# Attention scores in one round over four banks, x standardised by GpSimd, the gate bias over 128 rows, and a new order at the end of a step

## The chip, the cores and the metric

The kernel runs on one core of a Trainium2 chip. The metric is the device time of one launch in microseconds; lower is better. Times of single operations below come from one profiled execution.

## The reference, cut to what matters

One transformer layer over 4096 tokens of 256 numbers: a gated linear attention with 16 heads of 16, and then a mixture of eight experts of which each token uses two.

```python
h = layernorm(x) * (1 + ca) + sa
q, k, v = h @ Wq, h @ Wk, h @ Wv                       # 16 heads of 16
g = log_sigmoid(h @ Wgk1 @ Wgk2 + bgk2) / 16
state_t = state_{t-1} * exp(g_t) + v_t k_t^T           # a scan over the tokens, for each head
o_t = state_t q_t
o = (layernorm(o) * gamma + beta) * silu(h @ Wg)
x = x + ga * (o @ Wout)
h2 = layernorm(x) * (1 + cb) + sb
w = softmax over the two best of (h2 @ Wr + br)        # eight experts
x = x + gb * sum_e w_e * (gelu(h2 @ W1[e] + b1[e]) @ W2[e] + b2[e])
```

## The kernel before, in words

The tokens are cut into 32 chunks of 128. The scan is done by chunks: inside a chunk as a masked product of scores with values, between chunks by a 256-wide state. The heads lie in four strips of 32 partitions (two heads in a strip for each of the two halves j of the 256 numbers).

The program is five instruction streams (SyncE, GpSimd, ScalarE, VectorE, TensorE). Each is written out by hand as a function `step(s, u, front, back, finish, route)`, and `walk` (line 412) calls it for s = -1 to 33. Steps 4 to 29 are a loop of 13 rounds with two steps each; the others are written out. Each engine works strictly in its own order, and semaphores bind the streams. In one step s four chunks are at different stages:

- front (chunk f = s+1): projections of h to gate and decay (`p_gz`, with a bias product of `ones_r` by `zb_r` over two rows), to q and k (`p_qk`) and to v (`p_v`), their transposes, and the cumulative sums of the decay (`p_cum`). Each float32 product of h is made as three of rounded parts. `hT_lo_r` (line 873, VectorE) is the low part of h.
- back (chunk s): scores (line 1125), their mask (line 863), outputs (line 1138), the update of the state.
- finish (chunk s-1): normalisation of the output (lines 880 and 883), the product with Wout, the residual x1 (line 911), and its standardisation into `rows` (line 956).
- route (chunk s-2): the router's scores (line 899), the two best experts (lines 901 to 921), places of rows (lines 965 to 985), and two indirect DMAs (line 635).
- nextx (chunk s+2): statistics of x (line 894), the inverse root on ScalarE (line 739), the standardised x on VectorE (line 928, whose instruction is recorded at line 809, tile `host_n`), its transposes on TensorE, and h on ScalarE (line 764).

PSUM has eight banks: `p_tr`, `p_qk`, `p_v`, `p_gz`, `p_cum`, `p_o` and the two of `p_s`. The scores of strips 0 and 1 are made in the two banks of `p_s`; VectorE masks them into SBUF (`mask(0)`); then the scores of strips 2 and 3 are made in the same two banks and masked (`mask(1)`). TensorE puts the gate projection between the two rounds. The last things on TensorE in a step are the transposes of x, the transposes of `rows` into `p_v`, the counts of the router into `p_cum`, and the transposes of the output into `p_o`.

After the 34 steps VectorE makes tables, and 64 to 72 tiles of 128 rows go through the experts. That stage reuses the same banks and is not touched.

In the rows, all products have line 1099 and the transposes 1118, so a tile's name tells them apart: `p_s<-w_all,qkT_both` are scores, `w_hi<-p_s,upto` is a mask, `host_n<-host_x,mv_x` is x standardised, `w_r<-hT,w_r` is the low part of h, `p_gz<-zb_r,ones_r` the bias product, and `w_all<-qkT_both,own_pair` (line 599, GpSimd) is `qbd`, the left operand of the next step's scores.

## Time and profile before

| | us |
|---|---|
| median of three runs | 957.5 (956.02 to 960.76) |
| the profiled execution's own time | 960.28 |
| its span, first to last instruction | 958.1 |
| TensorE busy | 877.5 (92%) |
| VectorE busy | 626.1 (65%) |
| ScalarE busy | 473.4 (49%) |
| GpSimd busy | 403.7 (42%) |
| mean granted TensorE clock | 0.965 |

The profile calls TensorE PE (its weight loads PEld), VectorE DVE, ScalarE ACT, GpSimd POOL and SyncE SP. A busy share is an average over stages with different limits; the steps of attention and the tiles of the experts have to be read apart. A PE row's time ends when its last result is written, so the time that an operation takes on TensorE is better read from one start to the next.

### The profile page before, as it was taken

The numbers are of one execution on the slowest core, as the hardware profiler recorded it, in microseconds if no ns is written. First come the engines' busy times: TensorE is split into PE (matmuls) and PEld (weight loads), VectorE is DVE, ScalarE is ACT, GpSimd is POOL, SyncE is SP. The second block draws the span as 40 slices with busy tenths as digits, with TensorE's granted clock in tenths as the row PEclk, the third lists the DMA queues.
The fourth block names the chain that finished last, engine by engine and source line by source line (L and its number), as shares of the span: only waits on it lengthen the run. The fifth ranks groups of instructions, "written<-read, shape, count | busy, mean of one in ns | idle before, by whom it ended". The sixth has DMA issues, their size and how long they took to land.

```text
span 958.1 us, 24566 instructions
## 1 busy us (share of the span) xinstructions
PE 877.5 (92%) x6743; PEld 751.3 (78%) x6744; DVE 626.1 (65%) x1478; ACT 473.4 (49%) x1425; POOL 403.7 (42%) x419
## 2 busy tenths in 40 slices
PE   5799999999999999998269999999999999999995
PEld 4477777777777777776269999999999999999994
DVE  2578888888888888886534747465474565645653
ACT  2366666666666666663134443444434444443441
POOL 2246555555555555554204343343334434243342
PEclk9699999999999999998579999999999999999997
DMA  6911111111111111111273222222222222222222
GB/s 238 379 57 58 47 55 56 49 47 52 48 56 56 42 53 50 50 51 41 76 277 65 39 45 34 45 40 39 45 34 45 40 39 40 39 45 40 40 36 25
DMA packets 51449, 62.64 MB, mean 65 GB/s; under 512 B 6274, under 2 KB 46932, under 8 KB 51284
## 3 DMA queue, kind: packets, MB, share of 16 engines
q1 hardware_dynamic: 38548, 44.36, 14.4%
q0 software_dynamic: 12864, 17.83, 10.9%
q8 instruction: 17, 0.28, 0.1%
q14 instruction: 20, 0.16, 0.1%
HBM read 38.91 MB, written 23.27 MB: 65 GB/s over the span
## 4 chain that ended last, share of the span: by engine, by line
PE 70%; DVE 13%; issue 10%; DVEq 2%; ACT 2%; DMA 1%; SPq 1%; POOL 0%; ACTq 0%; POOLq 0%
PE p_s L1099 24%; PE p_qk L1099 11%; PE p_gz L1099 10%; PE p_v L1099 9%; PE p_cum L1099 6%; PE p_o L1099 4%; PE p_tr L1099 2%; DVE rows L809 2%; DVE w_hi L867 2%; PE p_o L1118 2%; PE p_v L1118 1%; PE p_tr L1279 1%; DMA w_all<-in_L_wmod_dram 1%; DVE o_tok L970 1%; DVE host_s_r L1083 1%
## 5 line engine op out<-in xcount | busy, mean ns | idle before, releaser
L655 POOL DMA_INDIRECT out_dram<-x,tok x68 | 166.6, 2450 | 312.5 <-DVE x L1076 297.0
L674 ACT ACTIVATE h2T<-p_tr,mods 128x128 f32<-128x128 f32 x136 | 54.9, 454 | 259.0 <-PE p_tr L1279 246.4
L1099 PE MATMUL p_s<-w_all_r,host_s_r 128*128 x544 | 143.1, 405 | 2.9 <-DVE host_s_r L1083 2.9
L1099 PEld LDWEIGHTS p_s<-w_all_r,host_s_r 128*128 128x128 f32 x544 | 97.8, 190 | 20.8 <-issue 3.3
L599 POOL TENSOR_TENSOR w_all<-qkT_both,own_pair 128x512 f32<-128x512 f32 x32 | 33.2, 1037 | 139.0 <-ACT qkT_both L744 139.0
L867 DVE TENSOR_TENSOR w_hi<-p_s,upto 128x1024 f32<-128x1024 f32 x64 | 77.9, 1218 | 12.2 <-PE p_s L1099 12.2
L635 POOL DMA_INDIRECT expert_rows<-rows,pos x64 | 64.4, 1006 | 49.7 <-issue 32.3
L1072 DVE TENSOR_TENSOR ga<-p_s,b_all 128x256 f32<-128x256 f32 x68 | 28.8, 423 | 85.3 <-PE p_s L1099 85.1
L1099 PE MATMUL p_s<-w_all,qkT_both 32*128 32x256 f32 x512 | 73.9, 406 | 3.6 <-DVE w_hi L867 1.5
L1099 PE MATMUL p_qk<-h2T,host_x 128*128 128x128 f32 x544 | 68.3, 280 | 2.5 <-ACT h2T L674 1.0
L1099 PE MATMUL p_v<-h2T,host_x 128*128 128x128 f32 x544 | 67.1, 276 | 3.3 <-DVE qkT_both L1035 2.4
L1099 PEld LDWEIGHTS p_qk<-h2T,host_x 128*128 128x128 f32 x544 | 65.4, 196 | 3.4 <-issue 3.4
L1099 PEld LDWEIGHTS p_v<-h2T,host_x 128*128 128x128 f32 x544 | 63.6, 192 | 4.7 <-issue 4.1
L1099 PE MATMUL p_cum<-h2T,qkT_both 128*128 128x128 f32 x544 | 66.8, 276 | 0.0
L1099 PE MATMUL p_gz<-h2T,qkT_both 128*128 128x128 f32 x544 | 66.3, 275 | 0.0
L1099 PEld LDWEIGHTS p_cum<-h2T,qkT_both 128*128 128x128 f32 x544 | 64.0, 193 | 0.0
L1099 PEld LDWEIGHTS p_gz<-h2T,qkT_both 128*128 128x128 f32 x544 | 63.5, 192 | 0.0
L1069 DVE CAST tok<-ln_host 128x1 uint32<-128x1 f32 x68 | 10.4, 153 | 75.9 <-issue 75.9
L1099 PEld LDWEIGHTS p_s<-w_all,qkT_both 32*128 32x128 f32 x512 | 44.5, 186 | 17.9 <-DVE w_hi L867 8.4
L1099 PE MATMUL p_gz<-w_r 128*128 128x512 f32 x128 | 46.2, 443 | 12.7 <-DVE w_hi_r L848 7.6
L723 ACT ACTIVATE host_s<-p_gz 128x512 f32<-128x512 f32 x32 | 19.1, 598 | 54.6 <-PE p_gz L1099 54.6
L1099 PEld LDWEIGHTS p_gz<-w_r 128*128 128x128 f32 x128 | 21.3, 194 | 30.8 <-DVE w_r L873 10.6
(208 smaller groups left out, 2011.1 us busy)
## 6 DMA issues: line engine op xcount, KB each, us to landing
ln_host<-expert_rows SPq DMA_DIRECT2D x68, 136.0 KB
host_x<-in_L_attn_x_dram SPq DMA_DIRECT2D x64, 128.0 KB, 2.1
w<-in_L_ffn_W_dram SPq DMA_DIRECT2D x8, 1024.0 KB, 13.9
w_all<-in_L_ffn_W_dram SPq DMA_DIRECT2D x8, 1024.0 KB, 12.5
out_dram<-x SPq DMA_DIRECT2D x32, 128.0 KB, 1.7
w_all<-in_L_wmod_dram SPq DMA_DIRECT2D x1, 1536.0 KB, 6.7
expert_rows<-pad_rows SPq DMA_DIRECT2D x8, 136.0 KB
out_dram<-x,tok POOLq DMA_INDIRECT x68, 4.6
```

What stands on the lines that cost most here:

```text
L599: nc.gpsimd.tensor_tensor(qbd, qkT[v][:, 0:KD, :].unsqueeze(2).to_broadcast([P, KD, 2, P]), own_pair[:].unsqueeze(1).unsqueeze(3).to_broad ...
L635: nc.gpsimd.indirect_dma_start(out=scratch, out_offset=bass.IndirectOffsetOnAxis(ap=pos[u][:, j:j + 1], axis=0), in_=rows[u][:], in_offset ...
L655: nc.gpsimd.indirect_dma_start(out=out, out_offset=bass.IndirectOffsetOnAxis(ap=tok[u][:, 0:1], axis=0), in_=y_out[u][:], in_offset=None, ...
L674: last = A.activation(dst[:, j, :], src[:, j * P:(j + 1) * P], ACT.Identity, scale=mods[:, which + 2 + j:which + 3 + j], bias=mods[:, whic ...
L723: gate.then(A.activation(gz_e, p_gz[:], ACT.Abs))
L809: return V.tensor_scalar(dst, src, mv[:, 0:1], mv[:, 2:3], ALU.subtract, ALU.mult)
L867: V.tensor_tensor(am[:, 2 * j:2 * j + 2, :].rearrange("p g (h t) -> p (g h) t", t=P), p_s[:].rearrange("p (h t) -> p h t", t=P), upto[:].u ...
L970: bo.mark(V.tensor_tensor(o_tok[:], p_o[:, D:2 * D], e_pos[u][:], ALU.mult))
L1069: V.tensor_copy(tok[u][:], xs[slot][:, ID:ID + 1]).then_inc(m_tok, 1)
L1072: V.tensor_tensor(y_lo[:], p_a[u][:, D:2 * D], b2_all[:, bass.ds(e * D, D)], ALU.add).then_inc(m_y_lo, 1)
L1099: return nc.tensor.matmul(dst, lhsT, rhs, start=start, stop=stop, skip_group_check=True)
L1118: last = nc.tensor.transpose(dst[:, k * P:(k + 1) * P], src[:, k * P:(k + 1) * P], ident[:])
```

## The change

All four strips' scores are made in one round, with one semaphore count for each step. `p_s` becomes four banks, of which the third also serves as `p_cum` and the fourth as `p_v`. Mask 0 reads banks 0 and 1, mask 1 banks 2 and 3. The projection to v therefore waits for both masks. The bias product contracts over 128 rows, of which 126 are zero. GpSimd standardises x, as the first thing of its step. On TensorE the transposes of `rows` go to the end of the step, into `p_qk`, and the counts go to `p_gz`. The wait for `h2T` stands ahead of the projection to q and k.

```diff
-        p_s = ctx.enter_context(nc.psum_tensor("p_s", [P, 1024], F32))
+        p_s = ctx.enter_context(nc.psum_tensor("p_s", [P, 2048], F32))
         p_a = [p_s[:, 0:512], p_s[:, 512:1024]]
+        p_cum, p_v = p_s[:, 1024:1536], p_s[:, 1536:2048]
-        zb_r = sb("zb_r", [2, D], F32R)
+        zb_r = sb("zb_r", [P, D], F32R)
 # GpSimd
+            nc.gpsimd.tensor_copy(zb_r[:], state[:])      # zeros, in the setup
+            def norm_x_end(n, u):
+                wait_apart(pool, *([] if isinstance(n, int) and n < 2 else [(xT_ready, n - 1)]), (x_scale, n + 1))
+                nc.gpsimd.tensor_scalar(xn[u][:], x_in[u][:], mv_x[:, 0:1], mv_x[:, 2:3],
+                                        ALU.subtract, ALU.mult).then_inc(xn_ready, 1)
+            norm_x_end(0, 0)
 ...
             def step(s, u, front, back, finish, route):
+                if nextx:
+                    norm_x_end(s + 2, u)
                 if front:
                     pool.wait_ge(qkT_taken, f + 1)
-                    after(pool, a_ready, KD * f)
+                    after(pool, a_ready, f)
 # ScalarE
-                    modulate(h2T, p_v[:, D:2 * D], 4, h2T_ready)
+                    modulate(h2T, p_qk[:, 0:D], 4, h2T_ready)
 # VectorE
+                after(dve, xn_ready, n)                   # in norm_x, ahead of the statistics
                 def mask(j):
-                    dve.wait_ge(a_ready, KD * s + j + 1)
                     if j == 0:
                         after(dve, o_ready, s)
+                        dve.wait_ge(a_ready, s + 1)
 ...
-                                    p_s[:].rearrange("p (h t) -> p h t", t=P),
+                                    p_s[:, j * 1024:(j + 1) * 1024].rearrange("p (h t) -> p h t", t=P),
 ...
-                if nextx:
-                    norm_x_end(s + 2, u)
 ...
-                    V.tensor_tensor(slots[u][:], p_cum[:, 0:2 * E].rearrange("p (a e) -> p a e", a=2),
+                    V.tensor_tensor(slots[u][:], p_gz[:, 0:2 * E].rearrange("p (a e) -> p a e", a=2),
 # TensorE
-                def scores(r):
-                    if r == 0:
-                        after(pe, u_taken, s)
-                    else:
-                        pe.wait_ge(am_ready, KD * s + r)
+                def scores():
+                    if isinstance(s, int) and s == 0:
+                        pe.wait_ge(vn_ready, 1)
+                    after(pe, u_taken, s)
                     for j in range(KD):
-                        for b in range(2):
+                        for b in range(P // STRIP):
 ...
                 if back:
                     pe.wait_ge(qbd_ready, s + 1)
-                    scores(0)
+                    scores()
                 if front:
                     pe.wait_ge(hT_hi_ready, f + 1)
                     after(pe, silu_ready, f)
+                    after(pe, ranks_taken, s - 2)
                     project(p_gz[:], wgz_hi_r, wgz_r, False)
-                    mm(p_gz[:, D:2 * D], ones_r[0:2, :], zb_r[:], False, True).then_inc(gz_ready, 1)
-                if back:
-                    scores(1)
+                    mm(p_gz[:, D:2 * D], ones_r[:], zb_r[:], False, True).then_inc(gz_ready, 1)
+                if route:
+                    pe.wait_ge(h2T_ready, s - 1)
 ...
+                    if back:
+                        pe.wait_ge(am_ready, KD * s + 2)
                     project(p_v[:, 0:D], wv_hi_r, wv_r).then_inc(proj_ready, 1)
 ...
-                if finish:
-                    pe.wait_ge(xn2_ready, s)
-                    if front:
-                        pe.wait_ge(vn_ready, f + 1)
-                    transposes(p_v[:, D:2 * D], rows[v], KD, x2T_ready)
                 if route:
                     pe.wait_ge(hot_ready, s - 1)
                     if front:
-                        pe.wait_ge(e_ready, f + 1)
+                        pe.wait_ge(silu_ready, f + 1)
+                    else:
+                        pe.wait_ge(ranks_taken, s - 2)
 ...                                                       # the counts, now into p_gz
                 if back:
                     pe.wait_ge(oT_taken, s + 1)
                     transposes(p_o[:, D:2 * D], oT, KD, ot_ready)
+                if finish:
+                    pe.wait_ge(xn2_ready, s)
+                    if front:
+                        pe.wait_ge(qkT_taken, f + 1)
+                    transposes(p_qk, rows[v], KD, x2T_ready)
```

## Rows read from the trace of the kernel before

**Rows 1.** Windows by stage: length, busy us (instructions) by engine, clock, DMA share, GB/s
```profile
39.70:90.32 50.62, 49.66 (x391) 37.70 (x389) 37.05 (x93) 30.86 (x83) 22.49 (x33) 0.93 0.32 110
90.32:430.97 340.65, 323.88 (x2679) 247.08 (x2679) 280.35 (x807) 215.48 (x598) 186.06 (x261) 1.00 0.15 51
430.97:482.30 51.33, 27.23 (x192) 20.34 (x191) 31.42 (x109) 12.08 (x36) 16.86 (x24) 0.68 0.17 60
```

**Rows 2.** Windows of two steps of the loop, from scores to scores; same columns
```profile
206.95:219.70 12.75, 12.35 (x104) 9.53 (x103) 10.58 (x32) 8.26 (x24) 7.13 (x11) 1.00 0.15 53
219.70:233.24 13.54, 12.61 (x104) 9.46 (x103) 11.05 (x32) 8.35 (x24) 7.22 (x11) 1.00 0.16 50
```

**Rows 3.** Timeline of TensorE in these steps: start, length, engine, line, operation
```profile
209.65 0.38 PE L1099 MATMUL p_gz<-zb_r,ones_r 2*128 2x256 f32 x1
210.00 1.13 PE L1099 MATMUL p_s<-w_all,qkT_both 32*128 32x256 f32 x8
211.06 0.73 PE L1099 MATMUL p_qk<-w_r 128*128 128x512 f32 x2
...
226.67 0.96 PE L1099 MATMUL p_v<-w_r 128*128 128x256 f32 x6
```

**Rows 4.** Timeline of VectorE in these steps
```profile
207.09 0.42 DVE L970 TENSOR_TENSOR o_tok<-p_o,host_n 128x256 f32<-128x256 f32 x1
...
208.29 0.51 DVE L873 TENSOR_TENSOR w_r<-hT,w_r 128x256 fp32r<-128x256 f32 x1
208.73 1.21 DVE L867 TENSOR_TENSOR w_hi<-p_s,upto 128x1024 f32<-128x1024 f32 x1
...
221.41 0.93 DVE L873 TENSOR_TENSOR w_r<-hT,w_r 128x256 fp32r<-128x256 f32 x1 [0.32 <-issue]
222.27 1.21 DVE L867 TENSOR_TENSOR w_hi<-p_s,upto 128x1024 f32<-128x1024 f32 x1
...
224.71 1.22 DVE L867 TENSOR_TENSOR w_hi<-p_s,upto 128x1024 f32<-128x1024 f32 x1 [0.23 <-PE p_s L1099]
...
228.63 0.42 DVE L911 TENSOR_TENSOR x<-p_o,host_x 128x256 f32<-128x256 f32 x1 [1.16 <-PE p_o L1099]
...
229.44 0.16 DVE L921 TENSOR_TENSOR hot<-iota_e,top_i 128x16 bf16<-128x16 f32 x1
...
229.74 1.18 DVE L809 TENSOR_SCALAR host_n<-host_x,mv_x 128x256 f32<-128x256 f32 x1
...
231.90 0.57 DVE L809 TENSOR_SCALAR rows<-x,mv 128x256 f32<-128x256 f32 x1
```

**Rows 5.** Timeline of ScalarE in the second of these steps
```profile
227.68 0.20 ACT L685 ACTIVATE mv_x<-mv_x 128x1 f32<-128x1 f32 x1
...
229.85 0.29 ACT L684 ACTIVATE mv<-mv,eps 128x1 f32<-128x1 f32 x1 [0.29 <-DVE mv L926]
...
231.00 0.38 ACT L758 ACTIVATE host_n<-p_cum 128x256 f32<-128x256 f32 x1
```

**Rows 6.** Timeline of GpSimd in these steps
```profile
221.32 0.74 POOL L627 TENSOR_TENSOR host_s<-w_all,w 128x256 f32<-128x256 f32 x1
...
229.73 1.04 POOL L599 TENSOR_TENSOR w_all<-qkT_both,own_pair 128x512 f32<-128x512 f32 x1 [4.27 <-ACT qkT_both L744]
231.59 0.73 POOL L607 TENSOR_TENSOR ln_host<-w,gam 128x256 f32<-128x256 f32 x1 [0.82 <-DVE w L940]
```

**Rows 7.** Timeline of GpSimd and VectorE in step 30, where the two meet
```profile
438.95 1.04 POOL L599 TENSOR_TENSOR w_all<-qkT_both,own_pair 128x512 f32<-128x512 f32 x1 [3.49 <-ACT qkT_both L744]
...
439.14 0.88 DVE L921 TENSOR_TENSOR hot<-iota_e,top_i 128x16 bf16<-128x16 f32 x1
```

**Rows 8.** Timeline of GpSimd in the setup
```profile
3.57 0.56 POOL L569 TENSOR_SCALAR upto_half<-upto 128x128 f32<-128x128 f32 x1
...
26.10 1.30 POOL L590 TENSOR_TENSOR w_r<-w,w_r 128x512 fp32r<-128x512 f32 x1
```

**Rows 9.** Groups by line and shape: busy us, mean ns of one | idle before
```profile
L1099 PE MATMUL p_o<-w_hi,w 128*32 128x128 f32 x1024 | 35.4, 280 | 0.0
```

More of the change, by code:

```diff
@@ L81, in build @@
         p_qk = bank("p_qk")
-        p_v = bank("p_v")
         p_gz = bank("p_gz")
-        p_cum = bank("p_cum")
-        p_s = ctx.enter_context(nc.psum_tensor("p_s", [P, 1024], F32))
+        p_s = ctx.enter_context(nc.psum_tensor("p_s", [P, 2048], F32))
         p_a = [p_s[:, 0:512], p_s[:, 512:1024]]
+        p_cum, p_v = p_s[:, 1024:1536], p_s[:, 1536:2048]
         p_o = bank("p_o")
@@ L581, in _ @@
             nc.gpsimd.memset(eps[:], EPS)
-            nc.gpsimd.memset(state[:], 0.0)
+            order.then(nc.gpsimd.memset(state[:], 0.0))
             for r in rows:
                 nc.gpsimd.memset(r[:], 0.0)
+            nc.gpsimd.tensor_copy(zb_r[:], state[:])
             nc.gpsimd.memset(vbd[:], 0.0).then_inc(consts_made, 1)
             pool.wait_ge(consts_made, 1)
+            def norm_x_end(n, u):
[3 more added lines that the diff above has]
+            norm_x_end(0, 0)
             for n, (w, w_r, hi_r) in enumerate(((wqk, wqk_r, wqk_hi_r), (wv, wv_r, wv_hi_r))):
@@ L594, in step @@
                 f, v = s + 1, 1 - u
+                nextx = front and not (isinstance(s, int) and s + 2 >= NC)
+                if nextx:
+                    norm_x_end(s + 2, u)
                 if front:
                     pool.wait_ge(qkT_taken, f + 1)
-                    after(pool, a_ready, KD * f)
+                    after(pool, a_ready, f)
                     nc.gpsimd.tensor_tensor(
@@ L816, in norm_x @@
                     dve.wait_ge(xin_loaded[u], (n - u) * 8 + 16)
+                after(dve, xn_ready, n)
                 statistics(ln, x_in[u][:], st_x, mv_x, x_stats)
-            def norm_x_end(n, u):
-                after(dve, xT_ready, n - 1)
-                standardise(xn[u][:], x_in[u][:], mv_x, n, x_scale).then_inc(xn_ready, 1)
             norm_x(0, 0)
-            norm_x_end(0, 0)
             dve.wait_ge(mod_ready, 1)
@@ L841, in _ @@
             setup.then(V.tensor_copy(zb_hi, zb))
-            setup.then(V.tensor_copy(zb_r[:], zb))
-            setup.then(V.tensor_scalar(zb_hi, zb_r[:].bitcast(F32), ident[0:2, 1:2], None, ALU.mult))
-            V.tensor_tensor(zb_r[:], zb, zb_hi, ALU.subtract).then_inc(gate_split, 1)
+            setup.then(V.tensor_copy(zb_r[0:2, :], zb))
+            setup.then(V.tensor_scalar(zb_hi, zb_r[0:2, :].bitcast(F32), ident[0:2, 1:2], None, ALU.mult))
+            V.tensor_tensor(zb_r[0:2, :], zb, zb_hi, ALU.subtract).then_inc(gate_split, 1)
             for n, (w, at) in enumerate(((wgz[:, :, 0:D], slice(0, D)),
@@ L1123, in step @@
                 nextx = front and not (isinstance(s, int) and s + 2 >= NC)
-                def scores(r):
-                    if r == 0:
-                        after(pe, u_taken, s)
-                    else:
-                        pe.wait_ge(am_ready, KD * s + r)
+                def scores():
+                    if isinstance(s, int) and s == 0:
+                        pe.wait_ge(vn_ready, 1)
+                    after(pe, u_taken, s)
                     for j in range(KD):
-                        for b in range(2):
-                            at = slice((2 * r + b) * STRIP, (2 * r + b + 1) * STRIP)
-                            last = mm(p_a[b][:, j * 2 * P:(j + 1) * 2 * P], qkT[u][at, KD + j, :],
+                        for b in range(P // STRIP):
+                            at = slice(b * STRIP, (b + 1) * STRIP)
+                            last = mm(p_s[:, b * 512 + j * 2 * P:b * 512 + (j + 1) * 2 * P], qkT[u][at, KD + j, :],
                                       qbd[at, j, :, :].rearrange("p h t -> p (h t)"), True, True)
@@ L1196, in step @@
                 if route:
-                    pe.wait_ge(h2T_ready, s - 1)
                     for j in range(KD):
@@ L1215, in step @@
                     after(pe, e_ready, f)
-                    after(pe, ranks_taken, s - 2)
                     if isinstance(s, int) and s < 0:
@@ L1242, in step @@
                     if front:
-                        pe.wait_ge(e_ready, f + 1)
+                        pe.wait_ge(silu_ready, f + 1)
+                    else:
+                        pe.wait_ge(ranks_taken, s - 2)
                     for n, counts in enumerate((before_b, ones_b)):
                         for k in range(TOP):
-                            last = mm(p_cum[:, n * E:(n + 1) * E], counts[:], hot[:, k, :], k == 0, k == TOP - 1)
+                            last = mm(p_gz[:, n * E:(n + 1) * E], counts[:], hot[:, k, :], k == 0, k == TOP - 1)
                     last.then_inc(rank_ready, 1)
```

## The prediction

> **What bounds the kernel now.** I read the busy shares by stage first [rows 1]. The loop over chunks is 26 steps in 340.65 us, 13.10 us a step, with TensorE busy for 323.88 us of it (95%) at full clock. The steps before the loop take 50.62 us from the gate product of step 0 on, those after it 51.33 us. The expert stage behind them takes the other half of the span; the change leaves its instructions alone, so the gain or loss has to come from the 35 steps.
>
> The windows of two steps [rows 2] show that the steps alternate, 12.75 and 13.54 us. TensorE is busy 12.35 and 12.61 us in them, VectorE 10.58 and 11.05, ScalarE 8.3, GpSimd 7.2. So TensorE is nearly full, but VectorE is close behind. A saving on TensorE alone cannot be worth more than its way down to what VectorE and the hand-overs allow. That second bound has to be worked out; most of this text is about it.
>
> The timeline of VectorE shows two kinds of hand-over. The 1.16 us of idle time ahead of x1 (228.63, "<-PE p_o") are VectorE waiting for TensorE's product with Wout. The 0.57 us from 231.90 on are `rows`, and TensorE waits for it before the transposes [rows 4]. Neither engine is free: each waits once a step for the other.
>
> The timeline also shows that VectorE is held up by GpSimd. The standardisation of x takes 1.18 us (229.74 to 230.92), while GpSimd's `qbd` runs from 229.73 to 230.77 [rows 4, 6]: it ends 0.15 us after GpSimd's instruction does. `rows` (231.90 to 232.47) ends 0.15 us after GpSimd's 231.59 to 232.32. The low part of h takes 0.93 us (221.41 to 222.34) and ends 0.28 us after GpSimd's instruction that ends at 222.06; in the other step it takes 0.51 us. In step 30 even the tiny `hot` (0.16 us elsewhere) takes 0.88 us, from 439.14 to 440.02, beside `qbd` from 438.95 to 439.99 [rows 4, 7]. The pattern: a VectorE instruction that reads two SBUF tensors, or a tensor_scalar from SBUF to SBUF, waits until the GpSimd instruction in flight is done.
>
> **The change part by part.**
>
> *Scores in one round.* A round of two strips is 8 matmul records and takes TensorE 1.06 us, from 210.00 to the next product at 211.06 [rows 3]. Four strips in four banks run beside each other if the array allows it. The trace has that only for column strips: 1024 records of `p_o<-w_hi,w`, four at a time, with 35.4 us of busy time, so 0.138 us for each group of four of which one record lasts 280 ns [rows 9]. For row strips the trace shows two at a time. Bounds: 1.06 us for the new round (four beside each other) and 2.12 us (two beside two). I take 1.06, the nearer behaviour of the column strips. That removes one round, 1.06 us of TensorE a step.
>
> *The bias over 128 rows.* The two-row product costs 0.35 us from start to start (209.65 to 210.00) for 256 columns [rows 3]. It is entered and left like a scores round, with no overlap of weight load and product. As a plain 128-row product of 256 columns it should cost what the v projection pays for one, 0.96 us for six overlapping, some 0.12 to 0.15 us. I take 0.11 to 0.24 us saved, and 0.1 us each for the wait in front of it and for the first q-k product that no longer follows scores. Bounds 0 and 0.45 us together; I take 0.42.
>
> TensorE's own floor is then 12.35 - 1.06 - 0.42 = 10.87 us a step, 2.2 under today's mean.
>
> *x standardised by GpSimd.* VectorE loses 1.18 us a step, all of it between `hot` and the weights. GpSimd gets one tensor_scalar of 128x256. The trace has none of that shape: 0.56 us for 128x128 from below, 1.30 us for a two-input instruction of 128x512 from above [rows 8]. I take 0.80. It starts when ScalarE's root is ready (227.68 + 0.20) plus about 0.17, which is how long `qbd` waits behind ScalarE. GpSimd was idle for 4.27 us ahead of 229.73 [rows 5, 6], so it costs GpSimd's order nothing: `qbd`, queued behind it, is released by ScalarE 1.8 us later. The indirect DMAs of the step before are behind it by then: the 4.27 us of idle time begin after them. Without that cover, each 0.1 us of delay of `qbd` would reach the next scores only after GpSimd's last 2 us of slack ahead of them are gone.
>
> What it may cost is VectorE's `hot`. Counted from the end of mask 1 (225.93), the root ends at +1.95 us and the new instruction at +2.12 + its length. The projection to v now starts at the end of mask 1, and x1 follows it after 1.96 us (226.67 to 228.63), `hot` after another 0.81 (to 229.44) [rows 3, 4], so `hot` starts at +2.82. Up to 0.7 us (0.87 with hand-overs counted closely) the GpSimd instruction is out of its way; beyond that each 0.1 us costs the step 0.1 us. At 0.80 I book nothing, and 0.1 to 0.6 us in the range.
>
> The Trainium skill speaks against this edit: "GPSIMD Engine Reference", sections Specifications and Key points, says that GpSimd shares its SBUF interfaces with VectorE and contends with two-port modes and with instructions of two SBUF inputs. The four holds above are that rule at work here (0.15 to 0.28 us after GpSimd's end). By it the move can give part of its 1.18 us back, which is the third rival below.
>
> *The new waits.* The v projection waits for both masks, and behind it on TensorE are the product with Wout, the q-k transposes, sums and outputs. This is the one added wait that I expect to decide. The cycle from v to v, from one step to the next, is then:
> - v start to x1 start, 226.67 to 228.63: 1.96 [rows 3, 4]
> - x1 start to the end of the third exponential, which passes through VectorE's statistics, ScalarE's root (229.85) and four more activations, 228.63 to 231.38: 2.75 [rows 4, 5]. Today the 1.18 us instruction hides behind this chain; taking it out brings the value product forward by only 0.14 us.
> - the value product and its hand-over, ahead of `rows`: 0.38
> - `rows`, state and places: 0.41 to 0.57 for `rows`, 0.47 for the other two at the spacing of such instructions; I take 0.90
> - output, statistics and places, 207.09 to 208.29: 1.20 [rows 4]
> - the low part of h to mask 0: 0.44 (208.29 to 208.73) or, behind GpSimd, 0.86 (221.41 to 222.27) [rows 4]
> - mask 0 and the output's normalisation, 222.27 to 224.71 less the 0.23 us of waiting and the usual overlap of 0.1: 2.1 [rows 4]
> - mask 1 and the hand-over: 1.22 + 0.05
>
> With 0.86 the sum is 11.42 us, with 0.44 it is 11.00. GpSimd's state products come at about the moment at which VectorE is ready for the low part, and every second step VectorE loses 0.32 us at the loop's branch ("issue" at 221.41) [rows 4], which puts it right into them. I take 11.40. This is 0.5 above TensorE's floor, so TensorE will wait about 0.5 us for masks, mainly ahead of v.
>
> *The order at the end of a step.* Today `rows` holds up the counts and the transposes of the output behind it on TensorE. Afterwards these two go first, and the transposes of `rows` come last, with the next scores behind them; the scores need the state sum, which VectorE makes after `rows`, so nothing that could start earlier is held. The wait for `h2T` ahead of q-k has the scores and the gate product (some 2.7 us) as cover for ScalarE's 0.8 us. Cost nothing; without that cover 0.8 us at most.
>
> *Setup and ends.* GpSimd's extra copy of 128x256 (0.3 to 0.6 us) is over before the loads are. Step 0 waits for the first value product, up to 1.2 us. Steps 0 to 3 then gain like the others: 3.5 us together. Steps 31 to 33 lose one scores round and take over step 30's lead, partly at the lower clock of 1.2 GHz (granted 0.68 in that window [rows 1]): 2 us, between 0 and 5.
>
> **The sum.** 26 x (13.10 - 11.40) = 44.2, and 3.5 + 2: 49.7 us. The profiled execution's own time is 960.28 us, 2.2 more than its span, so 910.6. It lies 2.8 us above the median of the runs, so on their scale 907.8; I say 908.
>
> **The rivals.**
> - *Two strips at a time.* If four row strips do not run beside each other, the round costs 2.12 us and TensorE's floor is 11.93 a step. For it: no row of the trace shows four row strips. Against: the column strips. Gain 26 x 1.17 + 4 = 34: 923.
> - *TensorE decides.* The low part of h is never held, and the cycle falls to TensorE's floor or just above, 10.95. Gain 26 x 2.15 + 6 = 62: 896. For it: GpSimd's and VectorE's chains meet within some 0.1 us. Against: the loop's branch. The Trainium skill ("TensorE: Matmul & The Clock Gate", section Measured speedup vs the span model) has four row tiles at 3.07 times one, so an estimate of 4/3.07 = 1.3 for the length of a group; the round would be 1.38 us, the floor 11.19, and this rival 902. No row here shows four row strips.
> - *GpSimd holds `hot`.* The GpSimd instruction takes 1.30 us, the upper bound. The step is 11.8 to 11.9, gain 26 x 1.25 + 5 = 38: 920.
> - *Slower.* The same mechanism with a long instruction: from 0.87 us on it adds its whole excess to each of the steps, since `hot`, the statistics, ScalarE's root, the exponentials and the next masks are all behind it; the lead of 1.7 us is used up at 2.6 us. At 3.0 us the step is 13.5 and the time 12 us more: 970. For it: a tensor_scalar with two scalars from memory is in no row of GpSimd. Against: its two-input instructions of 128x256 take 0.73 and 0.74 us [rows 6].
> - *The change doesn't do what it says:* an overlap of banks would force waits that aren't written; the semaphores that are written are the ones I counted. I give it nothing of its own.
>
> **How the numbers follow.** Forecast 0.62, two strips 0.10, TensorE decides 0.11, `hot` held 0.12, slower 0.03, and 0.02 for a loss of the gain that I don't see. The likeliest gives 908. The range goes from 895 to 924, which takes in the first three rivals. A measurement here tells about 0.5% (5 us) from no change. Faster 0.95, same 0.02, slower 0.03.
>
> **What would show it.** The steps of the loop 11.3 to 11.5 us apart, and hardly alternating. Scores as one row of 16 records within 1.2 us (2.1 if the first rival holds). An idle stretch of TensorE ahead of `p_v` put down to the mask, some 0.5 us a step. A GpSimd row `host_n` of 0.7 to 0.9 us, over before `hot`; `hot` at 0.16 us (0.5 or more if it is held). The low part of h at 0.9 us in at least one of two steps. The expert stage as long as before, 475 us. The prediction is wrong if the steps come out above 11.9 or under 11.0, or if the expert stage moves.

## The result and the profile after

The changed kernel takes 902.7 us (median of 4 runs, 902.04 to 903.19) where the kernel before takes 957.6 (956.02 to 960.76). The ratio is 0.9422, 95% interval 0.9398 to 0.9447: 55 us less. A second measurement gave 903.5, ratio 0.9426 (0.9413 to 0.9439). The forecast was 908, in 895 to 924. The cycle that was to set the step did so, and the gain was 11% larger than forecast. What the forecast made of two parts, the new order and x on GpSimd, was wrong; the last sections come back to both.

The profiled execution took 902.91 us, its span is 901.1 (958.1 before). Windows of the changed kernel by stage (length, busy us and instructions of PE, PEld, DVE, ACT, POOL, clock, DMA share, GB/s): steps 0 to 3, the loop of 26 steps, the last steps, the expert stage; and two steps of the loop.

```profile
39.29:83.65 44.36, 43.12 (x389) 34.97 (x389) 33.13 (x86) 30.31 (x82) 27.18 (x35) 0.96 0.38 130
83.65:376.69 293.04, 286.56 (x2679) 233.55 (x2679) 246.65 (x781) 215.66 (x599) 221.10 (x287) 1.00 0.18 59
376.69:427.00 50.31, 25.15 (x200) 19.26 (x199) 32.22 (x113) 13.28 (x40) 18.83 (x27) 0.69 0.18 63
427.00:901.00 474.00, 454.68 (x3400) 428.57 (x3400) 261.00 (x437) 203.28 (x681) 166.92 (x68) 0.98 0.28 52
196.52:207.87 11.35, 11.00 (x104) 8.88 (x104) 9.35 (x31) 8.13 (x24) 8.20 (x11) 1.00 0.19 59
207.87:219.05 11.18, 11.03 (x105) 9.09 (x104) 9.59 (x31) 8.47 (x24) 8.81 (x13) 1.00 0.18 60
```

These windows run from the start of one scores round to another. Those of [rows 1] run from the gate product behind it, some 1.1 us later. The loop went from 340.65 us [rows 1] to 293.04: 47.6 of the 57.0 us of span, 11.27 us a step instead of 13.10. It starts at 83.65; in the kernel before its first scores start at 89.18. That is 5.5 us, and 3.9 are left for what comes after it. The expert stage is as long as before (474.00 us in the fourth window, 475 forecast): from its first transposition to the end it takes 473.1 us (from 428.01), before 473.5 (from 484.57). The steps hardly alternate now (11.35 and 11.18, against 12.75 and 13.54 [rows 2]). TensorE is busy 97 to 99% of each.

TensorE in these steps (start, length, engine, line, operation, idle before it and what ended it). The rows answer to [rows 3]:

```profile
201.81 0.98 PE L1106 MATMUL p_s<-w_r 128*128 128x256 f32 x6 [0.35 <-DVE w_hi L876]
...
207.87 1.15 PE L1106 MATMUL p_s<-w_all,qkT_both 32*128 32x256 f32 x16
208.94 0.73 PE L1106 MATMUL p_gz<-w_r 128*128 128x512 f32 x2
...
210.44 0.28 PE L1106 MATMUL p_gz<-zb_r,ones_r 128*128 128x256 f32 x1
210.55 0.63 PE L1106 MATMUL p_qk<-w_r 128*128 128x512 f32 x2
...
212.16 0.51 PE L1106 MATMUL p_tr<-wr,h2T 128*128 128x8 f32 x4
212.68 0.97 PE L1106 MATMUL p_s<-w_r 128*128 128x256 f32 x6
```

All sixteen records of scores stand in one row. The next product starts 1.07 us after them, and eight records took 1.06 [rows 3]: four row strips run beside each other at no extra time. The bias costs 0.11 us from start to start (0.35 before [rows 3]). The name `p_s<-w_r` is the v projection, since its bank is now a quarter of `p_s`. In one of the two steps 0.35 us of idle time stand ahead of it, put down to the mask. Read by starts, TensorE waits there in both steps. The router's scores `p_tr<-wr,h2T` in front of it took 0.36 us from start to start before (226.31 to 226.67). Here they take 0.52 (212.16 to 212.68) in the one step and 0.86 (200.95 to 201.81) in the other. The row itself lasts 0.51 us and hides 0.15 of each wait, so the waits are 0.16 and 0.50 us.

VectorE in these steps, answering to [rows 4]. The first three rows are of the step that has the loop's branch in it:

```profile
196.22 0.41 DVE L977 TENSOR_TENSOR o_tok<-p_o,host_n 128x256 f32<-128x256 f32 x1
...
197.79 0.70 DVE L882 TENSOR_TENSOR w_r<-hT,w_r 128x256 fp32r<-128x256 f32 x1 [0.33 <-issue]
198.41 1.21 DVE L876 TENSOR_TENSOR w_hi<-p_s,upto 128x1024 f32<-128x1024 f32 x1
...
203.79 0.42 DVE L920 TENSOR_TENSOR x<-p_o,host_x 128x256 f32<-128x256 f32 x1 [0.49 <-PE p_o L1106]
...
204.59 0.16 DVE L930 TENSOR_TENSOR hot<-iota_e,top_i 128x16 bf16<-128x16 f32 x1
...
205.75 0.15 DVE L940 TENSOR_SCALAR wt<-gap_e 128x1 f32<-128x1 f32 x1 [0.78 <-ACT gap_e L762]
...
206.91 0.48 DVE L822 TENSOR_SCALAR rows<-x,mv 128x256 f32<-128x256 f32 x1
...
207.72 0.41 DVE L977 TENSOR_TENSOR o_tok<-p_o,host_n 128x256 f32<-128x256 f32 x1
...
208.88 0.39 DVE L882 TENSOR_TENSOR w_r<-hT,w_r 128x256 fp32r<-128x256 f32 x1
209.19 1.22 DVE L876 TENSOR_TENSOR w_hi<-p_s,upto 128x1024 f32<-128x1024 f32 x1
...
211.40 1.22 DVE L876 TENSOR_TENSOR w_hi<-p_s,upto 128x1024 f32<-128x1024 f32 x1
```

ScalarE's third exponential, answering to [rows 5]:

```profile
206.15 0.38 ACT L771 ACTIVATE host_n<-p_s 128x256 f32<-128x256 f32 x1
```

GpSimd in the same steps, answering to [rows 6]:

```profile
203.75 1.23 POOL L593 TENSOR_SCALAR host_n<-host_x,mv_x 128x256 f32<-128x256 f32 x1 [1.39 <-ACT mv_x L698]
204.95 1.03 POOL L612 TENSOR_TENSOR w_all<-qkT_both,own_pair 128x512 f32<-128x512 f32 x1
...
208.97 0.90 POOL L638 TENSOR_TENSOR w_all<-host_s,w 128x256 f32<-128x256 f32 x1
```

Four things are to be seen. The projection to v starts right behind the end of mask 1 in both steps: 201.81 behind 201.76 (200.54 + 1.22, a row that is not shown), 212.68 behind 212.62 (211.40 + 1.22). GpSimd's x instruction takes 1.23 us, far more than the 0.80 that I took. `hot` (204.59 to 204.75) lies fully inside it and still takes 0.16 us, so it is not held. And where VectorE used to standardise x, it now waits 0.78 us for ScalarE (205.75).

### The profile page after: what moved, and what is told of

It is laid out like the page before. It is cut to its first block, busy times and chain, and to the rows that moved or that the text cites. A ratio compares the mean times of both kernels' runs of the same rounds, so it can differ in the third digit from the quotient of the medians.

```text
span 901.1 us, 24612 instructions
## 1 busy us (share of the span) xinstructions
PE 829.5 (92%) x6743; PEld 732.8 (81%) x6744; DVE 586.9 (65%) x1446; ACT 473.8 (53%) x1425; POOL 447.6 (50%) x452
## 4 chain that ended last, share of the span: by engine, by line
PE 75%; DVE 10%; issue 5%; ACT 4%; DVEq 2%; DMA 1%; SPq 1%; POOL 0%; ACTq 0%; POOLq 0%
PE p_s L1106 42%; PE p_gz L1106 10%; PE p_qk L1106 8%; PE p_o L1106 8%; DVE w_hi L876 4%; PE p_qk L1125 2%; PE p_tr L1106 2%; PE p_tr L1288 2%; ACT h2T L687 1%; ACT hT L687 1%; PE p_o L1125 1%; DVE host_o L889 1%; DMA w_all<-in_L_wmod_dram 1%; PE p_tr L1125 1%; DVE host_s_r L1090 1%
## 5 line engine op out<-in xcount | busy, mean ns | idle before, releaser
L1106 PE MATMUL p_s<-h2T,host_x 128*128 128x128 f32 x544 | 67.1, 276 | 3.8 <-DVE qkT_both L1042 2.8
L1106 PEld LDWEIGHTS p_s<-h2T,host_x 128*128 128x128 f32 x544 | 63.6, 192 | 5.2 <-issue 4.5
L1106 PE MATMUL p_s<-h2T,qkT_both 128*128 128x128 f32 x544 | 66.3, 275 | 0.0
L593 POOL TENSOR_SCALAR host_n<-host_x,mv_x 128x256 f32<-128x256 f32 x32 | 39.2, 1225 | 53.2 <-ACT mv_x L698 53.2
L1106 PEld LDWEIGHTS p_s<-h2T,qkT_both 128*128 128x128 f32 x544 | 63.5, 192 | 0.0
L1092 DVE TENSOR_TENSOR host_o_r<-host_o,host_s_r 128x1024 fp32r<-128x1024 f32 x34 | 41.7, 1225 | 1.2
L1092 DVE TENSOR_TENSOR host_n_r<-host_n,host_s_r 128x1024 fp32r<-128x1024 f32 x34 | 41.7, 1225 | 1.2
L787 ACT ACTIVATE host_n<-p_qk,b_col 128x128 f32<-128x128 f32 x136 | 38.9, 370 | 6.1 <-issue 6.1
```

What stands on the lines that cost most here:

```text
L593: nc.gpsimd.tensor_scalar(xn[u][:], x_in[u][:], mv_x[:, 0:1], mv_x[:, 2:3], ALU.subtract, ALU.mult).then_inc(xn_ready, 1)
L787: last = A.activation(act[slot % 2][:, k * P:(k + 1) * P], hidden[slot % 2][k // 4][:, k % 4 * P:(k % 4 + 1) * P], ACT.Gelu_apprx_tanh, bi ...
L1092: V.tensor_tensor(act_r[1 - u], act[1 - u], act_hi_r.bitcast(F32), ALU.subtract).then_inc(m_lo, 1)
L1106: return nc.tensor.matmul(dst, lhsT, rhs, start=start, stop=stop, skip_group_check=True)
```

## The experiments

"Gain" is 957.6 x (1 - ratio), so that chips compare; half the interval is 1.5 to 2.4 us with 4 runs and 1.2 to 1.6 with 5. The step is the loop's length over 26, from one profiled execution. T1, T2 and T3 are the theories that were written down before each run, as quoted.

| kernel | us | ratio (95%) | gain | step |
|---|---|---|---|---|
| changed | 902.7 | 0.9422 (0.9398-0.9447) | 55.3 | 11.27 |
| x on VectorE again | 904.8 | 0.9426 (0.9401-0.945) | 55.0 | 11.42 |
| bias over 2 rows again | 905.8 | 0.9441 (0.942-0.9461) | 53.5 | 11.36 |
| old order again | 920.1 | 0.9584 (0.9564-0.9604) | 39.8 | 11.84 |
| all three again | 923.4 | 0.9645 (0.9623-0.9667) | 34.0 | 12.04 |
| before + order | 936.3 | 0.9771 (0.9748-0.9794) | 21.9 | 12.40 |
| before + x on GpSimd | 950.5 | 0.9922 (0.99-0.9945) | 7.5 | 12.86 |
| v after the first mask | 901.6 | 0.9391 (0.9374-0.9408) | 58.3 | 11.25 |
| TensorE +0.43 us a step | 908.0 | 0.9479 (0.946-0.9497) | 49.9 | 11.47 |
| TensorE -0.47 us a step | 898.4 | 0.9388 (0.9373-0.9404) | 58.6 | 11.18 |
| v after mask, x mixed | 899.9 | 0.9388 (0.9375-0.9401) | 58.6 | 11.24 |

**x on VectorE again.**
```
-                nc.gpsimd.tensor_scalar(xn[u][:], x_in[u][:], mv_x[:, 0:1], mv_x[:, 2:3], ...)   # GpSimd, first in its step
+                standardise(xn[u][:], x_in[u][:], mv_x, n, x_scale).then_inc(xn_ready, 1)        # VectorE, behind hot
```


> The changed kernel with one part undone: VectorE standardises x again, at its old place behind the statistics of x1. Changed kernel: 902.7 us, loop step 11.27 us, VectorE idle 0.78 us a step ahead of the weights (row wt). Theory 1 (one cycle through VectorE, ScalarE and TensorE sets the step): 0.78 us of the 1.18 us fall into that idle time, and the rest delays rows, state sum and masks by 0.2 to 0.4 us a step: 908 to 914. Theory 2 (TensorE's own work sets the step, and each part of the change is worth what it takes from TensorE): no change, 902 to 904. Theory 3 (VectorE's work alone sets the step): the full 1.18 us a step, 935 to 940.

The window of its loop, columns as above:

```profile
81.71:378.58 296.87, 289.75 (x2680) 233.59 (x2679) 271.05 (x807) 215.62 (x599) 188.25 (x261) 1.00 0.18 59
```

No change that can be measured (0.9426 against 0.9422), so T2 comes nearest and T1 and T3 fall. The loop's step is 0.15 us longer, which is the 0.14 that the prediction gave to this part. The loop is 3.8 us longer in all. It starts 1.9 us earlier, though (81.71 against 83.65), and that pays half of it back. T2's reason, that TensorE's own work sets the step, falls with the two runs on TensorE's work below. Most of the earlier start comes from step 0. Windows of the larger part of it, first of the changed kernel, then of this one:

```profile
39.29:48.00 8.71, 8.54 (x51) 6.87 (x55) 4.58 (x7) 4.58 (x11) 2.87 (x5) 0.80 1.05 379
```
```profile
38.92:48.00 9.08, 8.68 (x86) 7.21 (x87) 5.24 (x10) 5.43 (x14) 3.70 (x7) 1.00 1.05 380
```

The granted clock is 0.80 in the first and 1.00 in the second. From its scores to those of step 1, step 0 takes 10.91 us in the changed kernel and 9.57 in this one. TensorE's timeline of the changed kernel there: it waits for GpSimd's new instruction and then for `qbd` behind it.

```profile
38.29 0.44 PE L1125 MATMUL p_tr<-ident,host_n 128*128 128x128 f32 x2 [1.34 <-POOL host_n L593]
39.29 1.15 PE L1106 MATMUL p_s<-w_all,qkT_both 32*128 32x256 f32 x16 [0.57 <-POOL w_all L612]
40.37 1.20 PE L1106 MATMUL p_gz<-w_r 128*128 128x512 f32 x2
```

The gate product then takes 1.20 us for 0.73 us in the loop (208.94 above), which is the lower of the clock's two levels (1.2 GHz).

GpSimd's instruction alone does not bring the lower clock. The run with the old order, further down, has x on GpSimd too, and its step 0 has the clock at 1.00 and takes 9.57 us:

```profile
39.36:48.00 8.64, 8.25 (x82) 6.66 (x83) 5.00 (x8) 5.50 (x14) 4.15 (x6) 1.00 1.05 380
```

What differs is how long TensorE sat idle ahead of the transposes of x: 1.02 us there, and 0.31 in the run with less TensorE work, which has the clock at 1.00 too. In the changed kernel and the four other runs with an idle time of 1.33 or 1.34 us the clock of step 0 is 0.80 to 0.81. But the kernel before has 0.35 us and still only 0.62, so the idle time is not the whole of it, and no run isolates the cause.

**Bias over 2 rows again.**
```
-                    mm(p_gz[:, D:2 * D], ones_r[:], zb_r[:], False, True)
+                    mm(p_gz[:, D:2 * D], ones_r[0:2, :], zb_r[:], False, True)      # zb_r of 2 rows
```


> The changed kernel with the bias product over two rows again. Theory 1 (the cycle through VectorE sets the step; TensorE has 0.13 to 0.35 us of waiting ahead of the v projection as cover): 0 to 0.15 us a step, 903 to 907. Theory 2 (TensorE's work sets the step): two changes of the array's shape come back, 0.35 to 0.42 us a step, 913 to 916.

The window of its loop:

```profile
83.99:379.22 295.23, 292.64 (x2680) 233.17 (x2679) 246.49 (x781) 215.08 (x599) 220.67 (x287) 1.00 0.18 59
```

T1. TensorE's busy time rises by 6.1 us over the loop (292.64 against 286.56), 0.23 a step; the loop grows by 2.2. Most of a TensorE saving is not passed on. The 1.8 us between the two gains are within the intervals; the loop's 2.2 us are of one execution each.

**Old order again.**
```
+                if finish:  pe.wait_ge(xn2_ready, s) ... transposes(p_qk, rows[v], KD, x2T_ready)   # here, ahead of counts
                 if route:   ... counts into p_gz
                 if back:    ... transposes(p_o[:, D:2 * D], oT, KD, ot_ready)
-                if finish:  ...                                                                   # and no longer last
```


> The changed kernel with the transposes of rows ahead of the router's counts and the transposes of the output, as in the kernel before (banks stay as changed). Both theories: the counts and the output's transposes wait for rows, TensorE idles 0.3 to 0.4 us there and VectorE's output product starts as much later: 0.4 us a step, 914 to 918. If the order is worth nothing, 902 to 904.

The order is worth 15.5 us, not the nothing that the prediction booked, and 2 us more than the upper end of what was expected here. The timeline of this kernel around the end of a step, first TensorE's transposes of `rows` and its gate product, then VectorE's rows:

```profile
200.90 0.44 PE L1125 MATMUL p_qk<-ident,rows 128*128 128x128 f32 x2 [0.18 <-DVE rows L822]
...
204.31 0.73 PE L1106 MATMUL p_gz<-w_r 128*128 128x512 f32 x2 [0.42 <-DVE w_r L882]
```
```profile
200.36 0.48 DVE L822 TENSOR_SCALAR rows<-x,mv 128x256 f32<-128x256 f32 x1
...
201.46 0.17 DVE L972 TENSOR_TENSOR slots<-p_gz,slots 128x16 f32<-128x16 f32 x1 [0.28 <-PE p_gz L1106]
201.73 0.42 DVE L977 TENSOR_TENSOR o_tok<-p_o,host_n 128x256 f32<-128x256 f32 x1
...
203.34 0.92 DVE L882 TENSOR_TENSOR w_r<-hT,w_r 128x256 fp32r<-128x256 f32 x1 [0.33 <-issue]
```

TensorE stands at the rows' transposes, the counts stand behind them, and VectorE waits 0.28 us for the counts. From `rows` to `o_tok` it is 1.37 us here and 0.81 in the changed kernel (206.91 to 207.72). The half microsecond more then pushes the low part of h into GpSimd's instruction (0.92 us instead of 0.70), and TensorE waits 0.42 for it.

**All three again: the round alone.**

> The changed kernel with x on VectorE, the bias over 2 rows and the old order of the tail all put back: what is left is the scores in one round and the new banks. T1 (parts overlap: without the new order VectorE's 1.18 us for x stand on the cycle, a step of 12.1 us against 11.84 with the order alone undone): 924 to 930. T2 (parts add: 902.7 + 15.5 for the order + 1.8 for the bias + 0 for x): 919 to 922. T3 (the single round is worth little by itself and the order nearly everything): 940 or more.

923.4 lies between T1 and T2, nearer to T1. The single round, with its banks, is worth 34.0 us, and its step 12.04 is 1.06 below that of before, as much as the TensorE time of the round removed.

**Before + order.**
```
-                if finish: ... transposes(p_v[:, D:2 * D], rows[v], KD, x2T_ready)    # ahead of the counts
                 ... counts, oT
+                if finish: ... transposes(p_v[:, D:2 * D], rows[v], KD, x2T_ready)    # last
```


> The kernel before with one part of the change: TensorE transposes the finished rows last in its step instead of ahead of counts and oT; banks and rounds as before. T1 (TensorE's queue stood at the rows while slots and the next hi split waited behind; undoing the order in the changed kernel cost 15 us): 13 us less, 943 to 947. T2 (the order pays only with the scores in one round, since in the kernel before the mask between two rounds decides): 955 to 960. T3 (the router of the next step gets its rows later and its scores are late): 962 or more.

The window of its loop:

```profile
87.53:409.80 322.27, 318.07 (x2679) 246.66 (x2679) 274.11 (x807) 213.05 (x599) 188.31 (x261) 1.00 0.16 54
```

T1's direction, but more: 21.9 us. TensorE is busy 318.07 us of the loop's 322.27 (99%). In the kernel before, its waits in the loop are 10.5 us for `rows` (26 times) and 5.2 us for the low part of h (12 times); both are gone here. The 12.40 a step are thus nearly all TensorE's own work, close to the 12.35 of [rows 2]. That an edit on VectorE's side would be worth nothing behind this one is to be expected, but no run here shows it.

**Before + x on GpSimd.** The same move as in the change, with banks, rounds and order as before.

> The kernel before with one part of the change: x is standardised by GpSimd instead of VectorE; banks, rounds, bias and order as before. T1 (VectorE is on the cycle of the kernel before, so its 1.18 us ahead of the route's weights and rows count in part): 7 us less, 949 to 953 where the kernel before has 957.5. T2 (the instruction runs in an idle stretch of VectorE, as undoing it in the changed kernel suggested, where it was worth 0): 956 to 960. T3 (the 1.2 us in front of GpSimd's qbd delay the next scores): 965 or more.

T1: 7.5 us. Where VectorE was on the cycle the move paid. Behind the new order it pays nothing that can be measured. The three parts one by one on the kernel before (34.0 + 21.9 + 7.5) would be 63.4; together with the bias they give 55.3.

**v after the first mask.** The prediction's critical wait taken away: v goes into a bank that the first mask frees, VectorE's value product reads it there, and the sums wait for the second.
```
-                        pe.wait_ge(am_ready, KD * s + 2)
-                    project(p_v[:, 0:D], wv_hi_r, wv_r).then_inc(proj_ready, 1)
+                        pe.wait_ge(am_ready, KD * s + 1)
+                    project(p_a[1][:, 0:D], wv_hi_r, wv_r).then_inc(proj_ready, 1)
...
+                        pe.wait_ge(am_ready, KD * s + 2)                            # ahead of the sums
```


> The changed kernel with the v projection in the second bank of the scores, which only mask 0 reads: v waits for mask 0 alone, and the cumulative sums behind it wait for mask 1. Theory 1: the cycle v, x1, exponentials, value product, masks, v is cut by one mask (1.2 us); TensorE's floor of 11.0 us is left: 0.15 to 0.25 us a step less, 894 to 898. Theory 2: TensorE's waits ahead of v were all that it did not work, the same 894 to 898 or a little less of it. If the masks' wait only moves on to the sums or to the output's transposes: 901 to 904.

The lesser case: the wait moves on. The waits of TensorE in the loop (total us, times, longest), first of the changed kernel, then of this one:

```profile
PE p_s L1106 <- DVE w_hi L876: 4.5, 13, 0.4
```
```profile
PE p_qk L1125 <- DVE rows L822: 1.3, 8, 0.2
```

The wait for the mask is gone. In its place TensorE waits for `rows` ahead of their transposes, which now stand right in front of the next scores. The loop is 0.6 us shorter in all (11.25 a step). The cycle that is left runs from `rows` over their transposes, the scores, gate and q-k products to v, mostly through TensorE's own work. By the loops of the two kernels it is only 0.02 us shorter than the one through the masks (11.25 and 11.27). That accounts for this run; that it is this cycle is read from the one wait above and not tested by itself.

**More and less TensorE work.** Each changes TensorE's work alone.
```
+                    for k in range(KD):      # x's and the rows' transposes issued twice into the same place
+                        nc.tensor.transpose(p_tr[:, k * P:(k + 1) * P], xn[u][:, k * P:(k + 1) * P], ident[:])
...                                          # and the same with rows[v], into p_qk
```


> The changed kernel with more work on TensorE alone: the transposes of the next x and of the finished rows are issued twice into the same place, four more transposes a step, by the distance of starts in the timeline (two in 0.22 us) 0.43 us a step; the output is the same. T1 (TensorE, 11.02 us busy of 11.27 a step, now decides nearly alone): 0.4 a step, 914 to 918. T2 (hand-overs among VectorE, ScalarE and TensorE decide as before, TensorE's 0.25 us of idle take a part and the rest adds where it is in their way): 0.15 to 0.25 a step, 907 to 911.


```
+                        if n == 1 and not whole:     # gate projection without its middle product
+                            continue
```


> The changed kernel with less work on TensorE alone: of the gate projection (p_gz) the middle one of the three products of the split operands is left out, so its output lacks that correction; 0.47 us a step less by the distance of starts in the timeline, nothing else changes. T1 (TensorE decides alone): 0.45 a step, 888 to 892. T2 (hand-overs decide: v and the sums wait for the masks instead, and the step stays where it is but for a part): 0 to 0.2 a step, 896 to 903.

T2 in both. 0.43 us more make a step 0.20 longer. 0.47 us less make it 0.09 shorter, and the mask's wait ahead of v comes in every step (waits of TensorE in the loop of this kernel):

```profile
PE p_s L1106 <- DVE w_hi L876: 9.0, 26, 0.4
```

So TensorE's 98% is not the bound. The cycle of hand-overs is, at 11.2 to 11.3 us, with TensorE's busy time 0.2 to 0.3 below. Of the 0.43 us more, the rows' second transposes (0.21) stand right ahead of the scores, on the cycle, and the step grew by as much; the x's do not. That fits, but each of the two was not run alone.

**Which GpSimd instruction holds which of VectorE's.** Measured by itself.

> Leaves the whole layer out: 16 phases, each 16 VectorE instructions of one kind (tensor_scalar 128x256, tensor_tensor 128x256, tensor_tensor 128x16 in bf16, bn_stats of 128x256) beside GpSimd idle, or beside 6 GpSimd instructions of 128x256 of one kind (tensor_scalar, tensor_copy, tensor_tensor); all f32. T1 (a GpSimd instruction with two tensor inputs stops VectorE, one with a single tensor input doesn't): beside tensor_tensor VectorE's own tensor_tensor and the tiny one are held to the ends of GpSimd's (over 1 us at least once each), beside tensor_scalar and copy they are as with GpSimd idle within 0.05 us, and GpSimd's tensor_scalar stays at 1.2 us. T2 (any GpSimd instruction stops any VectorE instruction with two inputs): held beside all three. T3 (GpSimd's 1.22 us were themselves stretched by VectorE): GpSimd's tensor_scalar takes 0.8 us or less where VectorE has finished.

The timeline of VectorE and GpSimd (16 and 6 instructions a phase; `none`, `scal`, `copy`, `tens` at the end of a VectorE name is what GpSimd does beside it):

```profile
30.17 5.45 DVE L113 TENSOR_TENSOR vtensgnone<-xa,xb 128x256 f32<-128x256 f32 x16
...
35.66 6.05 DVE L113 TENSOR_TENSOR vtensgscal<-xa,xb 128x256 f32<-128x256 f32 x16
35.73 9.47 POOL L91 TENSOR_SCALAR gscal<-xa,sc 128x256 f32<-128x256 f32 x6 [5.43 <-DVE vtensgnone L113]
...
45.30 6.64 DVE L113 TENSOR_TENSOR vtensgcopy<-xa,xb 128x256 f32<-128x256 f32 x16 [3.60 <-POOL gscal L91]
45.33 3.32 POOL L93 COPY gcopy<-xa 128x256 f32<-128x256 f32 x6
...
51.98 8.62 DVE L113 TENSOR_TENSOR vtensgtens<-xa,xb 128x256 f32<-128x256 f32 x16
52.03 5.27 POOL L95 TENSOR_TENSOR gtens<-xa,xb 128x256 f32<-128x256 f32 x6 [3.38 <-DVE vtensgcopy L113]
60.64 1.45 DVE L115 TENSOR_TENSOR vtinygnone<-small 128x16 bf16<-128x16 f32 x16
...
72.75 4.26 DVE L115 TENSOR_TENSOR vtinygtens<-small 128x16 bf16<-128x16 f32 x15 [0.23 <-issue]
...
82.48 7.23 POOL L91 TENSOR_SCALAR gscal<-xa,sc 128x256 f32<-128x256 f32 x6 [5.31 <-DVE vstatgnone L117]
...
95.17 5.32 DVE L117 BATCH_NORM_STATS2 vstatgtens<-xa 128x6 f32<-128x256 f32 x16
95.22 4.14 POOL L95 TENSOR_TENSOR gtens<-xa,xb 128x256 f32<-128x256 f32 x6 [3.27 <-DVE vstatgcopy L117]
```

T1 holds for GpSimd's tensor_tensor and nearly for its tensor_scalar, but not for its copy. Beside GpSimd's two-input instruction VectorE's two-input ones lose much: sixteen take 8.62 us for 5.45, the tiny ones 4.26 (fifteen) for 1.45. Beside its tensor_scalar they take 6.05 for 5.45 and 1.90 for 1.45. T1's bound of 0.05 us was too tight, there is a small hold. Beside its copies, which have one input as well, they take 6.64 for 5.45 and 2.68 for 1.45. For each microsecond that both engines run, VectorE's tensor_tensor loses 0.60 us to GpSimd's tensor_tensor (3.17 in 5.27), 0.36 to its copy (1.19 in 3.32) and 0.10 to its tensor_scalar (0.60 in 5.98). So the number of GpSimd's inputs does not tell the hold; the kind of instruction has to be measured. VectorE's one-input statistics aren't held: 5.32 us for sixteen, also beside the tensor_tensor. T3 falls: six of GpSimd's tensor_scalar take 7.23 us beside the statistics, 1.21 each, and 1.58 each on the mean beside VectorE's tensor_tensor. They are stretched there, but never short.

**A better version.** v after the first mask, and x on VectorE in the steps written out ahead of the loop, on GpSimd in the loop:
```
+                if nextx and isinstance(s, int):      # VectorE, as before the change
+                    norm_x_end(s + 2, u)
+                if nextx and not isinstance(s, int):  # GpSimd
+                    norm_x_end(s + 2, u)
```


> Both leads together: v into the bank that the first mask frees (as in e4), and x standardised by VectorE in the six steps written out ahead of the loop and by GpSimd in the loop. T1 (with x on VectorE the scores of the head start without GpSimd's 1.2 us in front of qbd, TensorE stays at its full clock there, and the head is 2 us shorter; the loop stays at 11.25 a step): 898 to 900. T2 (in e4 the head was already shorter, the two gains are one): 901 to 902. T3 (both within the noise of the changed kernel): 902 to 904.

> The changed kernel itself once more, on the same chip as the one beside it: 902 to 904.

T1: 899.9 against 903.5 on the same chip, and the intervals of the two ratios (0.9375 to 0.9401, 0.9413 to 0.9439) lie apart. Its loop starts at 81.49 (83.65 in the changed kernel) and takes 292.30 us, 0.7 less. The granted clock of its step 0 is 1.00.

## Why the prediction was right, and where it was off

- *Scores in one round:* right. 1.07 us for four strips, as for two. "Two strips at a time" is out, and the 1.38 us for the round that the second rival goes by did not come either.
- *The bias:* 0.24 us from start to start, the upper end of what I gave it. The product in front is 0.09 shorter (210.44 - 209.97 = 0.47 for 0.56) and the first q-k product 0.10. But undoing the bias cost only some 2 us (1.8 by the ratios, 2.2 in the loop) in 26 and more steps, since TensorE's waits take up the rest.
- *TensorE's floor:* 10.87 forecast, 11.00 and 11.03 busy. The booked terms add up from start to start (1.06 + 0.24 + 0.09 + 0.10 = 1.49 for 1.48). By starts the forecast holds. A step before takes 12.72 us (206.99 to 219.71) with 0.56 of waiting for `rows`, so 12.16, and less 1.49 that is 10.67. The step from 207.87 to 219.05 takes 11.18, of which 0.16 are the wait ahead of v, 0.10 are lost ahead of the q-k transposes and 0.26 around the transposes of `rows` at its end, and 10.66 are left. The busy time covers most of such waits, since a row lasts to its last result; the 0.15 come from there. What the 0.26 are, no row says.
- *x on GpSimd:* the instruction's length was mis-sized (0.80 taken, 1.23 measured), and the consequence was wrong as well. By the prediction's rule 0.36 us beyond 0.87 should have been added to each step, 9 us in the loop. `hot` was not held. The prediction let every GpSimd instruction hold two-input ones, because the four holds that it had [rows 4, 6, 7] were all beside GpSimd instructions with two inputs. (The fourth, `hot` in step 30, ends 0.03 us after GpSimd's instruction, not 0.15 to 0.28.) That the two errors cancelled is luck; the rival with `hot` held (920) had its condition met and still didn't come. The Trainium skill, "SBUF — State Buffer", section SBUF: two separate sides, says that of a GpSimd instruction and a VectorE instruction with two SBUF inputs the one that starts first has the shared pair of ports for its whole length, and that the other blocks. With GpSimd's tensor_tensor the runs agree, with its tensor_scalar they don't (VectorE loses 0.60 us in 5.98 us of it, and `hot` takes its usual 0.16 us inside one); the measurement decides.
- *The cycle, v to v, by its terms.* Forecast, then the step from 201.81 to 212.68, then the one with the branch. v to x1 1.96 | 1.98 | 2.07. x1 to the third exponential 2.75 | 2.74 | 2.75. Value product 0.38 | 0.38 | 0.37. `rows` to `o_tok` 0.90 | 0.81 | 0.88. `o_tok` to the low part 1.20 | 1.16 | 1.24 and 0.33 of branch. The low part 0.86 | 0.31 | 0.62. Masks and normalisation 3.37 | 3.49 | 3.40. Sums 11.42 | 10.87 | 11.66, mean 11.27, which is the loop's step. The branch's step is put together from 196.22, 197.79, 198.41 and the masks behind them, and for its other terms from the same rows one step later in the timeline.
- *The term that was mis-sized* is the low part of h. I took it as held to 0.86 us in every step; it is 0.47 on the mean. In one of two it starts 0.09 us ahead of GpSimd's instruction (208.88 and 208.97) and takes 0.39 us. In the other it meets it at the branch, as forecast, but is held for less (0.70). Against these 0.39 us stands the loop's branch, 0.33 us in one of two steps (0.16 a step), which I named but gave no term in the sum. The two partly cancel, which is luck again. GpSimd's hold did not go away with the low part either: in the step without the branch it falls on the first half of the output's normalisation, which takes 0.65 us at 210.32 instead of 0.47, and is in the 3.49. A step of 11.27 for 11.40 is 3.4 us in the loop.
- *The new wait* decided, as forecast: v starts 0.05 or 0.06 us after mask 1 in both steps. The wait is shorter than the 0.5 in each, 0.50 us in one of two steps and 0.16 in the other. Taking it away brought only 3 us, since another cycle lies right behind it. The prediction had not looked at that one.
- *The order* was booked as "cost nothing", and that is the step that failed in attribution. It is worth 15.5 us here and 21.9 alone. The sum came out right because the cycle was written down with the places right behind `rows` (0.90), where the kernel before, by the timeline of its VectorE, has 1.45:

```profile
218.36 0.57 DVE L809 TENSOR_SCALAR rows<-x,mv 128x256 f32<-128x256 f32 x1
...
219.81 0.42 DVE L970 TENSOR_TENSOR o_tok<-p_o,host_n 128x256 f32<-128x256 f32 x1
```

The gain lay in the term without being named.
- *Ends:* 5.5 for 3.5 and 3.9 for 2. Steps 0 to 3 got 6.2 us shorter (50.5 to 44.4) and started 0.6 later. The prediction's own terms, four steps at 1.7 less 1.2 for step 0, give 5.6; the 3.5 has no working. Step 0 would be 1.3 us better with the clock kept (9.57 for 10.91).
- *TensorE decides* (896) is out by the two runs with more and less work. *Slower* had a long GpSimd instruction as its condition; even 1.23 us cost nothing.

## What to carry to other kernels

Sum a cycle along its hand-overs, and compare each term with the same stretch of the kernel before: a gain can hide in a term. Undo each part alone and also do each alone, since a move that pays 7 us on one kernel pays nothing behind another edit. When a wait is removed, write down the cycle that is next; here it was 0.02 us a step away. And read TensorE's waits from start to start, since the end of a row can cover a part of them.

## What the runs showed of the hardware

- Four row strips of 32 rows in f32 take the time of two (1.07 us for 16 records, 1.06 for 8).
- On GpSimd a tensor_scalar of 128x256 f32 with two per-row scalars takes 1.21 us, a tensor_tensor 0.69 and a copy 0.35 (7.23, 4.14 and 2.11 us for six, beside VectorE's statistics, which are not slowed). The tensor_scalar has a single tensor to read and is the slowest.
- When both engines run two-input instructions back to back, they take turns: GpSimd's six take 5.27 us for 4.14, VectorE gets through six of its sixteen meanwhile, and through the other ten in the 3.3 us behind.
- VectorE's two-input instructions are held beside GpSimd's copies too (6.64 us for sixteen, 5.45 with GpSimd idle), and hardly beside its tensor_scalar (6.05).
- VectorE's bn_stats, with one input, is not touched by any of the three GpSimd kinds (5.32 to 5.33 us for sixteen in all). Its tensor_scalar is (7.80 us for sixteen beside GpSimd's tensor_tensor, 5.25 with GpSimd idle).
- In the five runs where TensorE sat idle for 1.33 or 1.34 us ahead of the transposes of x, the granted clock of step 0 was 0.80 to 0.81 and the step took 10.9 to 11.3 us. In two runs with the same GpSimd instruction but 1.02 and 0.31 us of idle time it was 1.00, and the step took 9.57 and 9.12 us.
